# Capsule routing: factors spread by single-precision products over 32 rows, and a third tap on GpSimd

## What is computed

```python
patches = patches.reshape(N, F_in, in_len, Ho, Wo, kh, kw)
priors = jnp.einsum('nfdhwij,ofijud->nhwofiju', patches, weight)
priors = priors.reshape(N, Ho, Wo, F_out, F_in * kh * kw, out_len)
logits = jnp.zeros_like(priors)
for r in range(3):
    probs = jax.nn.softmax(logits, axis=-3)
    out = jnp.sum(probs * priors, axis=-2, keepdims=True)
    if r != 2:
        out = squash(out)
        logits = logits + jnp.sum(priors * out, axis=-1, keepdims=True)
out = squash(jnp.squeeze(out, axis=-2))
```

## Time and profile before

| | us |
|---|---|
| median of three runs | 13064.68 |
| their range | 13056.39 to 13068.2 |
| the profiled execution: its own time | 13060.79 |
| its span, from the first to the last instruction | 13059.0 |
| around the span | 1.8 |
| mean granted TensorE clock, share of full speed | 0.982 |

### The profile page before, as it was taken

The page is one execution under the profiler, slowest core; times in us unless marked ns, Lnnn a source line. Parts: engine busy times, 40 slices in busy tenths (PEclk is TensorE's granted clock), DMA queues, the critical chain, the costliest instruction groups (busy, mean ns, idle before and its releaser), DMA issues. The chain is left out here.

```text
span 13059.0 us, 258656 instructions
## 1 busy us (share of the span) xinstructions
PE 12449.1 (95%) x76092; PEld 5276.3 (40%) x76348; DVE 9722.8 (74%) x18034; ACT 7866.5 (60%) x14774; POOL 2684.0 (21%) x2692
## 2 busy tenths in 40 slices
PE   6999999999996499999999999999999999999899
PEld 3555555555553133333333333333333333333233
DVE  7888888888887577777777777777777777777311
ACT  4666666666665166666666666666666666666411
POOL 3454444544443000000000000000000000000143
PEclk9999999999998699999999999999999999999999
DMA  3101011010112523223222232332322323223255
GB/s 77 22 15 22 17 20 22 15 22 15 22 21 55 132 64 75 66 66 73 66 70 69 67 72 66 73 70 64 75 66 67 72 66 71 68 69 72 64 124 109
DMA packets 853225, 771.45 MB, mean 59 GB/s; under 512 B 587076, under 2 KB 621348, under 8 KB 840740
## 3 DMA queue, kind: packets, MB, share of 16 engines
q1 hardware_dynamic: 850468, 747.29, 25.4%
q10 hardware_dynamic: 1536, 8.39, 0.3%
HBM read 510.50 MB, written 244.96 MB: 58 GB/s over the span
## 5 line engine op out<-in xcount | busy, mean ns | idle before, releaser
L1503 DVE TENSOR_REDUCE a_big<-a_mp 128x1 f32<-128x512 f32 x8192 | 5222.3, 685 | 1816.0 <-PE a_mp L1337 1797.7
L1423 ACT ACTIVATE a_ex<-a_sc 128x512 f32<-128x512 f32 x8192 | 4426.4, 601 | 1937.6 <-PE a_sc L1325 1932.6
L1337 PE MATMUL a_mp<-a_ks,a_qs 108*128 108x512 bf16 x8192 | 3131.1, 383 | 39.9 <-DMA a_ks<-qk_parts 25.1
L1325 PE MATMUL a_sc<-a_qs,a_ks 111*128 111x512 bf16 x8192 | 3124.5, 383 | 6.8 <-ACT a_ex L1423 4.5
L849 DVE TENSOR_TENSOR r_prod<-r_pg,r_win 128x512 f32<-128x512 f32 x3584 | 2319.4, 683 | 416.5 <-PE r_pg L583 227.9
L1351 PE MATMUL a_po<-a_ex,a_va 128*32 128x512 f32 x16384 | 2183.0, 605 | 2.1 <-ACT a_oc L1429 0.7
L1239 POOL TENSOR_TENSOR a_pieces<-a_left,a_pieces 128x512 bf16<-128x512 f32 x256 | 295.5, 1154 | 7319.5 <-ACT a_pieces L1409 7319.5
L1325 PEld LDWEIGHTS a_sc<-a_qs,a_ks 111*128 111x128 bf16 x8192 | 794.9, 97 | 2477.6 <-ACT a_ex L1423 1767.0
L524 POOL TENSOR_TENSOR r_prod<-r_temp,r_win 128x512 f32<-128x512 f32 x1024 | 1214.7, 1207 | 1298.3 <-PE r_pl L632 568.3
L587 PE MATMUL r_pg<-r_ident,r_spread 128*128 128x128 f32 x9216 | 1196.7, 278 | 113.3 <-DVE r_prod L849 94.5
L587 PEld LDWEIGHTS r_pg<-r_ident,r_spread 128*128 128x128 f32 x9216 | 1004.9, 142 | 573.0 <-DVE r_prod L849 275.1
(11 more groups left out here) (192 smaller groups left out, 11795.2 us busy)
## 6 DMA issues: line engine op xcount, KB each, us to landing
a_qs<-qk_parts SPq DMA_DIRECT2D x768, 144.0 KB
a_ks<-qk_parts SPq DMA_DIRECT2D x768, 144.0 KB
qk_parts<-a_pieces SPq DMA_DIRECT2D x128, 768.0 KB, 5.0
f_t<-mixed SPq DMA_DIRECT2D x48, 1536.0 KB, 16.7
a_tw<-second SPq DMA_DIRECT2D x512, 128.0 KB, 3.1
mixed<-a_t SPq DMA_DIRECT2D x256, 256.0 KB, 2.1
r_win<-first SPq DMA_DIRECT2D x128, 280.5 KB, 5.2
a_zw<-layered SPq DMA_DIRECT2D x192, 144.0 KB, 12.2
```

The source lines that it names most:

```text
L1325: pe.matmul(sc[k % BANKS][:, :], ks[0:KROWS + NPART, p.h, head, 128 * kb:128 * kb + 128], qs[0:KROWS + NPART, p.h, head, CHUNK * qb:CHUNK ...
L1337: pe.matmul(mp[k % BANKS][:, :], qs[0:KROWS, p.h, head, 128 * q:128 * q + 128], ks[0:KROWS, p.h, head, CHUNK * half:CHUNK * half + CHUNK], ...
L1423: nc.scalar.activation(ex[:, k % RING, :], sc[k % BANKS][:, :], ACT.Exp, scale=scale).then_inc(exped.sem, 1)
L1503: nc.vector.tensor_reduce(big[:, x % 2, k // 2:k // 2 + 1], mp[k % BANKS][:, :], AX_X, ALU.max).then_inc(maxed.sem, 1)
```

## The change

- `POOLED` gets tap 6, `ORDER` becomes 4, 5, 0, 1, 6, 2, 3, 8, 7, and `AHEAD` 4. ACT then copies three factors a slot, and DVE has six products.
- Voting factors: the bf16 split goes. The vote is repeated four times (one ACT copy, `fourfold`), transposed in single precision and copied to `stack`, so that each group of 32 rows holds it. A factor is one single-precision matmul over the 32 rows of row group `use % RINGS`, the number of its bank.
- Summing factors: POOL multiplies the exponentials by a reciprocal (`rz`, an ACT exponential of minus the logarithm). The compact probabilities `pr` are transposed on PE in part C of the softmax, copied by ACT to `pr_t`, and spread over 128 rows by a matmul with a 0/1 table (`widen`) over the 32 rows of row group `tap % 4`. Tap 8 keeps four transposes, out of a tile that ACT writes with 512 elements (`pr_9`).
- The addition to the running vote in round 1 moves from DVE to POOL. POOL's products get a second buffer (`prod_2`, in odd slots), and its wait for the reduction is two slots back instead of one.

```diff
-ORDER = [4, 5, 0, 1, 2, 3, 8, 6, 7]
-POOLED = {4, 5}
+ORDER = [4, 5, 0, 1, 6, 2, 3, 8, 7]
+POOLED = {4, 5, 6}
-AHEAD = 5
+AHEAD = 4
...
             if voting:
-                w = slice(128 * tap, 128 * tap + 128)
-                pe.matmul(bank[:, :], wv_0[0:96, w], stack[0:96, lane, :], start=True, stop=False)
-                last = pe.matmul(bank[:, :], wv_12[:, w], stack[:, lane, :], start=False, stop=True)
+                q = slice(32 * (use % RINGS), 32 * (use % RINGS) + 32)
+                last = pe.matmul(bank[:, :], wv[q, 128 * tap:128 * tap + 128], stack[q, lane, :],
+                                 start=True, stop=True, tile_position=(32 * (use % RINGS), 0))
+            elif tap < 8:
+                q = slice(32 * (tap % 4), 32 * (tap % 4) + 32)
+                last = pe.matmul(bank[:, :], widen[q, tap // 4, :], pr_t[q, lane, :],
+                                 start=True, stop=True, tile_position=(32 * (tap % 4), 0))
             else:
...
+            elif part == "C":
+                pe.wait_ge(prob[r].sem, prob[r].at(n, lane + 1))
+                for b in range(BLK):
+                    last = pe.transpose(pt[:, 128 * b:128 * b + 128], pr[:, lane, 128 * b:128 * b + 128], ident[:, :])
+                last.then_inc(prob_turned[r].sem, 1)
...
             for d, kind, r, lane, part in lights(s, "C", ("softmax",)):
+                if d in which:
+                    n = p.to(d).n
+                    act.wait_ge(prob_turned[r].sem, prob_turned[r].at(n, lane + 1))
+                    nc.scalar.copy(pr_t[:, lane, :], pt[:, :]).then_inc(prob_copied[r].sem, 1)
+                    nc.scalar.copy(pr_9[:, lane, :, :], pr[:, lane, 512:576].unsqueeze(2).to_broadcast([128, 64, CLEN])
+                                   ).then_inc(ninth[r].sem, 1)
+            for g in own[2:]:
+                evacuate_make(g)
...
-                dve.wait_ge(squashed[1].sem, squashed[1].at(n, k))
-                nc.vector.tensor_tensor(vote[:, lane, :], vote[:, lane, :], sq[:, 1, lane, :], ALU.add).then_inc(voted[1].sem, 1)
```

More of the change, by code:

```diff
@@ L353, in routing_phase @@
     prod = sb("prod", [128, TAPS, CHUNK])
[L355 removed]
+    prod_2 = sb("prod_2", [128, len(POOLED), CHUNK])
     temp = sb("temp", [128, len(POOLED), CHUNK])
@@ L439, in routing_phase @@
     lz_ready = rounds("lz_ready", 2)
-    log_prob = rounds("log_prob", 2)
-    prob = [Signal(sem(f"prob{r}"), 3 * LANES) for r in range(2)]
+    rz_ready = rounds("rz_ready", 2)
+    prob = rounds("prob", 2)
+    prob_turned = rounds("prob_turned", 2)
+    prob_copied = rounds("prob_copied", 2, 1)
+    ninth = rounds("ninth", 2)
     turns = []
     for s in range(SLOTS):
-        for x in lights(s, "C", ("squash",)) + lights(s, "A"):
+        for x in lights(s, "C") + lights(s, "A"):
             d, kind, r, lane, part = x
-            if kind == "softmax":
+            if kind == "softmax" and part == "C":
+                turns.append((x, prob_copied[r], lane + 1))
+            elif kind == "softmax":
                 turns.append((x, shifted[r], lane + 1))
@@ new lines, in probabilities @@
+        def probabilities(n, r, lane):
+            pool.wait_ge(rz_ready[r].sem, rz_ready[r].at(n, lane + 1))
+            nc.gpsimd.tensor_tensor(pr[:, lane, :].rearrange("p (k o f) -> p k o f", o=CAPS, f=CAPS),
+                                    ex[:, lane, :].rearrange("p (k o f) -> p k o f", o=CAPS, f=CAPS),
+                                    over_capsules(rz[:, lane, :], 36), ALU.mult).then_inc(prob[r].sem, 1)
+        def slot(p, s, heavy, which):
+            own = sorted(POOLED, key=ORDER.index) if heavy else []
+            lit = [(p.to(x[0]).n, *x[1:4]) for x in lights(s, "B") if x[0] in which]
+            for g in own[:2]:
+                product(p, s, g)
+            for n, kind, r, lane in lit:
+                if kind == "softmax":
+                    denominators(n, r, lane)
+                elif r == 1:
+                    add_vote(n, lane)
+            for g in own[2:]:
+                product(p, s, g)
+            for n, kind, r, lane in lit:
+                if kind == "softmax":
+                    probabilities(n, r, lane)
@@ L685, in slot @@
             back = [x for x in lights(s, "C", ("squash",)) if x[0] in which]
+            turn = [x for x in lights(s, "C", ("softmax",)) if x[0] in which]
             front = [x for x in lights(s, "A") if x[0] in which]
@@ L795, in slot @@
                 finish_squash(p.to(d), r, lane)
+            for d, kind, r, lane, part in lights(s, "C", ("softmax",)):
+                if d in which:
[4 more added lines that the diff above has]
+                                   ).then_inc(ninth[r].sem, 1)
+            for g in own[2:]:
+                evacuate_make(g)
             for d, kind, r, lane, part in lights(s, "A", ("squash",)):
@@ L1872, in lay_out @@
             pick[p, t, 16 * t + p // CLEN] = 1
+    widen = np.zeros((LANES, 2, CAPS * CAPS, 2, CAPS * CAPS, CLEN), f)
+    for k in range(2):
+        for of in range(CAPS * CAPS):
+            widen[:, k, of, k, of, :] = 1
+    widen = widen.reshape(128, 2, 128)
     times = np.full(IMG, 3, f)
```

182 lines of the change are left out of this document (72 added, 110 removed).

## The result

| | kernel before | changed kernel |
|---|---|---|
| median | 13066.01 us (13056.39 to 13068.2) | 13624.99 us (13611.6 to 13649.67) |
| ratio | 1 | 1.0432 (95%: 1.0420 to 1.0445) |
| span of the profiled execution | 13059.0 us | 13621.6 us |
| routing, to its end | 4154.8 us | 4653.1 us |
| the rest, attention and fold, which the diff doesn't touch | 8904.1 us | 8968.4 us |

Slower, as forecast, but by 559 us where the forecast said 266. The two lower lines are worked out from the traces and hold the first surprise: 64 of the 559 us lie behind the routing, in code that is the same.

A forecast was written before the change was run, and what follows sets the result against it. PE was taken to set the slots, except four a pass held up by DVE's vote addition. Terms 12.5 - 3.2 + 1.7 - 2.7 = +8.3 us a pass, 32 passes, +266 on 13060.8, gave 13327 us; own range 13200 to 13420, overall 13000 to 14000.

The forecast's parts named there:

- the clock: Routing: PE priced at full 2.4 GHz; a granted clock under 0.98 would lengthen PE's work and wasn't in the sum.
- Summing slots +12.5: Eight slots a pass: matmul rounds, gaps, loads and probability transposes replace 36 transposes on PE; +12.5 us a pass.
- Voting slots -3.2: Eight slots a pass: nine matmuls over 32 rows replace 18 bf16 products on PE; -3.2 us a pass.
- The kept share: Voting slots: of 0.87 us saved on PE, 0.4 a slot stays, since PE comes to wait for DVE.
- Vote transposes +1.7: Vote transposed in single precision on PE: four cost 0.44 us instead of 0.23, eight times a pass; +1.7 us a pass.
- Addition off VectorE -2.7: Four slots a pass that add to the vote, 7.71 us against 6.88, get shorter; -2.7 us a pass.
- ScalarE and GpSimd at zero: Added work on ACT and POOL stays hidden under PE's slot; zero on the path.
- Turns by halves: Rival: neighbouring matmuls over 32 rows overlap by one half only; some 20 us a pass more, 13960 us; chance 0.11.
- no overlap at all: Rival: matmuls in different row groups run one after the other; about 62 us a pass more, 15050 us; chance 0.07.
- Half the price for 32 rows: Rival: a matmul over 32 rows costs 0.43 us; 10 us a pass gained, 12740 us; chance 0.07.
- No gap between modes: Rival: no drain between full array and row groups, voting slots keep 0.87 us; 13100 down to 13000 us; chance 0.14.
- GpSimd late: Rival: POOL's three products and softmax work use up its spare time; 4 us a pass, 13450 us; chance 0.11.

The follow-up runs named there:

- e5_shift: Changed kernel with 64 identity transposes on PE once after routing's last batch, ahead of the attention loop; 13560.1 us.
- e1_fill: Changed kernel with 16 more single-precision transposes on PE ahead of tap 8 in slot 14 of each pass, filling the pause; 13361.76 us.
- e12_fill_elsewhere: Changed kernel with 16 added transposes ahead of tap 8 in slot 12, where PE has no pause, instead of slot 14; 13606.59 us.
- e4: Kernel before with only the voting half changed (single-precision votes, one matmul over 32 rows a factor, vote addition on POOL); 13113.42 us, ratio 1.0042.
- e13: e1_fill with the third tap undone: taps 4 and 5 on POOL, the tap order of before, AHEAD 5; 13427.72 us.
- e14: e13 with DVE's products in voting slots over half the columns, the other half left out, as a test only; 13235.23 us.
- e10_addition: Kernel before with only the addition to the vote moved from DVE to POOL; 12981.57 us, ratio 0.9938.
- e6_before_shift: Kernel before with 16 identity transposes (32 instructions) on PE once after routing's last batch; 13133.85 us.
- e3_sum_only: Changed kernel with the voting half as before: bf16 products, votes split in three bf16 parts, vote addition on DVE; 13616.34 us.
- e11_third_tap: Kernel before with only the third tap on POOL (taps 4, 5, 6, new tap order); 13415.71 us, ratio 1.0272.

## Why the prediction was wrong in size

The forecast was 13327 us, the time 13625; it is inside the range of 13000 to 14000 and has the right sign. Without the first two rows of this table it would be 13362, inside the forecast's own range of 13200 to 13420. The 559 us come apart by runs:

| part | forecast | shown | by |
|---|---|---|---|
| stops in the attention loop | 0 | 72 (61 by the traces, the other 11 rather the clock's) | 13625 less 13553, e5_shift without its own 7 us |
| clock at 1.2 GHz after the pause | 0 | 191 | 13553 less e1_fill 13362 |
| all the rest, in routing | 266 (8.3 a pass) | 296 to 306 (9.3 a pass) | e1_fill less before |

**The step that failed** is the clock, which was put at nothing: every term was priced in time at 2.4 GHz, and a granted clock under 0.98 was named as what would make it wrong but got no term and no chance. The pause of about 2 us in slot 14 stood in the trace of before, and so did the 14 falls of 3.4 us behind it; the prediction names neither. What the runs showed in its place: a pause there, of 1.45 to 2.6 us, with the products over 32 rows behind it leaves the clock low (in the changed kernel 12.3 us a pass), and that costs 191 us (filling it, e1_fill, gives them back; the same fill in slot 12, e12_fill_elsewhere, doesn't). The second miss is that the unchanged part was taken as unmoved: the stops in the attention loop, 61 to 72 us, were no term and no rival.

**The terms**, per pass, from PE's start-to-start times by line in e1_fill and before (29 passes each):

- Summing slots +12.5: measured +12.7 (products, tap 8 and probabilities' transposes 48.2 us, against 35.6). Right, down to two rounds in either stretch.
- Voting slots -3.2: measured -4.6 (29.1 against 33.8). The kept share was 0.58 us a slot instead of 0.4. The reason given for keeping only a part, banks that the same products free, is the right one, and e4, e13 and e14 show it; what the prediction didn't see is that the part depends on the third tap. It priced that tap at zero on the path, and it is 5.1 to 5.3 us a pass through the banks.
- Vote transposes +1.7: measured +2.5 (4.7 against 2.2), and the transposes of the logits, not in the sum, +1.4 (5.8 against 4.4): a transpose ahead of or behind a stretch over 32 rows takes 0.49 to 0.59 where 0.44 was taken.
- Addition off VectorE -2.7: measured -2.5 alone (e10_addition); in the changed kernel it can't be told apart.
- These make +9.5; the pass of e1_fill is 9.3 us longer than before (the fill's 2.5 us in it stand where the pause was). The forecast's +8.3 was short by the transposes, 2.2, of which the voting slots gave back 1.4; that these two errors have opposite signs is luck.
- ScalarE and GpSimd at zero: right; PE waits for neither in the changed kernel.

**The rivals.** Turns by halves, and no overlap at all: no; eight instructions over four row groups are through in 1.14 us. The Trainium skill's rule behind the first (TensorE: Matmul & The Clock Gate, Part 3, strict order) doesn't hold between row groups in this trace: in program order they are two halves of one product, then two of the next, and that would take at least 2.15. In the stretch of four at 2105.74 the four first halves start within 0.02 us, and the second halves 0.53 later. Half the price for 32 rows: no, a round is 1.05 with its gaps. No gap between modes: no. GpSimd late: no.

## What to carry to other kernels

Read the granted clock around every pause of TensorE of 1.4 us and more, and ask what stands behind it after the change: nearly the same pause cost 0.8 us in every second pass here before and 6 us in each pass after, and 1.9 us of idle transposes put into it gained 191 us. Products spread over row groups arrive together, so the engine that empties their banks one by one sets the pace; count how fast banks return, not only how fast they fill. And when a diff holds several parts, price them alone: one line of this one, the addition moved to GpSimd is the version that beats both kernels (0.9938).

## What the runs showed of the hardware beyond that

- Matmuls of four row groups, single precision, overlap in full: 8 instructions in 1.14 us (one alone 1.12).
- Where a loop of TensorE begins in its program can cost 2.0 to 2.4 us a turn: 32 added instructions elsewhere made the kernel before 0.6% slower (e6_before_shift).
- An addition of 128x128 from SBUF to SBUF took 1.16 us on VectorE with GpSimd at work beside it, 0.29 us on VectorE in e3_sum_only, and 0.457 us on GpSimd.
- After a pause of 1.45 us the granted clock stood at 1.2 GHz for 10.2 or 13.7 us with single-precision products over 32 rows behind it (e3_sum_only), after one of 2.4 us for 3.4 us with dense transposes over 128 rows (25 of 32 passes of e11_third_tap).
